# Rotary embedding in quarters, and integer-weight casts on another engine, in a fused attention and FFN kernel

## The reference

```python
qkv = x @ W_qkv                                  # 1024 -> 3 * 1024
bq = bq * dh**-0.5;  bk, bv = look_around(...)   # window before + own window
bq = bq * cos + rotate_half(bq) * sin            # rotary embedding, q and k
bk = bk * cos + rotate_half(bk) * sin
sim = einsum('bhwid,bhwjd->bhwij', bq, bk);  mask;  attn = softmax(sim)
x = layernorm(x + (attn @ bv) @ W_out)
wg, wu, wd = (int32 weights) / 127               # HIDDEN = 3072
x = layernorm(x + (silu(x @ wg.T) * (x @ wu.T)) @ wd.T)
```

## Time and profile before

| | us |
|---|---|
| median of two runs (2235.42 and 2247.68) | 2241.55 |
| the profiled execution | 2229.26 |
| its span on the slowest core (core 1) | 2227.7 |
| spans of the 8 cores | 2201.4 to 2227.7 |
| PE busy in the span | 1789.0 (80%) |
| DVE busy | 630.6 (28%) |
| ACT busy | 528.9 (24%) |
| POOL busy | 345.4 (16%) |

### The profile page before, as it was taken

One profiled execution on the slowest core, in us unless ns is written; L12 is line 12 of the kernel. 1 busy time (PEld: TensorE's weight loads), 2 busy tenths in 40 slices (PEclk: granted clock), 3 DMA queues, 4 the chain that ended last, 5 costly groups with the idle time before them and its releaser, 6 DMA issues.

```text
span 2227.7 us, 27579 instructions; the slowest of 8 cores (2201.4 to 2227.7 us)
## 1 busy us (share of the span) xinstructions
PE 1789.0 (80%) x9568; PEld 789.5 (35%) x9568; DVE 630.6 (28%) x1000; ACT 528.9 (24%) x738; POOL 345.4 (16%) x549
## 2 busy tenths in 40 slices
PE   0075958686877969596599999999999999999992
PEld 0032323233323334243244444434444344444440
DVE  1013232333323232332311333132331423323212
ACT  2134242424233343424110211102111021120200
POOL 0122221313131222221000001020110202002022
PEclk9997989898977889898799999999999999999996
DMA  9874655556554546240424234252342523325251
GB/s 286 256 178 117 181 145 176 156 165 168 149 163 149 170 143 193 77 133 25 156 75 134 66 96 136 90 151 67 105 127 81 156 70 125 105 76 161 71 156 47
DMA packets 156088, 294.21 MB, mean 132 GB/s; under 512 B 22066, under 2 KB 41266, under 8 KB 155954
## 3 DMA queue, kind: packets, MB, share of 16 engines
q1 hardware_dynamic: 91442, 177.06, 27.1%
q10 hardware_dynamic: 46080, 65.03, 9.5%
q0 software_dynamic: 18432, 50.36, 7.5%
HBM read 231.54 MB, written 44.04 MB: 124 GB/s over the span
## 4 chain that ended last, share of the span: by engine, by line
PE 44%; issue 2%; ACT 1%; DVE 1%; DMA 1%; POOL 1%; SPq 0%; DVEq 0%; ACTq 0%; POOLq 0%
PE pg L995 14%; PE pu L1003 14%; PE pd L1044 8%; PE pg L1044 4%; PE pu L1044 4%; DMA wg_sb<-wg_sc 1%; PE pd L884 1%; PE pd L888 1%; DMA wd_buf<-wd_sc 1%; ACT L909 0%; POOL o L956 0%; DVE res L1055 0%; DVE rowsc L904 0%; DVE rows L894 0%; ACT rowsc L909 0%
## 5 line engine op out<-in xcount | busy, mean ns | idle before, releaser
L995 PE MATMUL pg<-y_sb,wg_sb 128*128 128x512 bf16 x1536 | 367.7, 382 | 33.1 <-DVE res L1055 14.9
L1003 PE MATMUL pu<-y_sb,wu_buf 128*128 128x512 bf16 x1536 | 364.5, 380 | 0.1
L1010 ACT ACTIVATE a_sb<-pg,consts 128x512 bf16<-128x512 f32 x192 | 131.2, 687 | 814.9 <-PE pg L995 814.8
L1015 DVE TENSOR_TENSOR h_sb<-a_sb,pu 128x512 bf16<-128x512 bf16 x192 | 131.3, 687 | 516.3 <-PE pu L1003 480.8
L440 PE MATMUL ps_ab<-x,wqk_buf 128*128 128x512 f16 x704 | 170.9, 393 | 126.0 <-ACT x L385 120.7
L995 PEld LDWEIGHTS pg<-y_sb,wg_sb 128*128 128x128 bf16 x1536 | 149.4, 98 | 223.4 <-issue 49.4
L956 POOL TENSOR_TENSOR o<-res,mbc 128x512 f32<-128x512 bf16 x64 | 75.1, 1174 | 933.1 <-ACT mbc L935 917.3
L1003 PEld LDWEIGHTS pu<-y_sb,wu_buf 128*128 128x128 bf16 x1536 | 150.6, 98 | 182.8 <-issue 2.8
L1044 PE MATMUL pd<-h_sb,wd_buf 128*128 128x512 bf16 x768 | 203.1, 387 | 1.9 <-DMA wd_buf<-wd_sc 1.5
L440 PEld LDWEIGHTS ps_ab<-x,wqk_buf 128*128 128x128 f16 x704 | 70.3, 101 | 215.7 <-issue 154.1
L706 PE MATMUL ps_ab<-q_sb,wqk_buf 128*128 128x512 f16 x512 | 128.9, 417 | 13.9 <-DVE q_sb L670 8.4
(11 more groups left out here) (115 smaller groups left out, 1813.8 us busy)
## 6 DMA issues: line engine op xcount, KB each, us to landing
wu_buf<-wu_sc SPq DMA_DIRECT2D x192, 256.0 KB, 2.6
wd_buf<-wd_sc SPq DMA_DIRECT2D x192, 256.0 KB, 3.5
wqk_buf<-wqk_sc SPq DMA_DIRECT2D x128, 256.0 KB, 3.4
x<-x_fm POOLq DMA_DIRECT2D x64, 256.0 KB, 4.8
wqk_buf<-wo_sc SPq DMA_DIRECT2D x64, 256.0 KB, 4.4
out_fm<-o POOLq DMA_DIRECT2D x64, 256.0 KB, 3.9
pin<-wgT ACTq DMA_DIRECT2D x48, 256.0 KB, 4.1
pin<-wu_shuf ACTq DMA_DIRECT2D x48, 256.0 KB, 4.0
```

Of the source, the lines that this page charges most:

```text
L995: g_last = P.op("pe", lambda e, hc=hc, dci=dci, gb=gb, yt=yt: e.matmul(out=pg[gb][:], lhsT=wg_sb[:, dci * HID + hc * 128: dci * HID + (hc ...
L1003: u_last = P.op("pe", lambda e, dci=dci, gb=gb, ub=ub, yt=yt: e.matmul(out=pu[gb][:], lhsT=wu_buf[:, ub * 1024 + dci * 128: ub * 1024 + (d ...
L1010: sl = P.op("act", lambda e, gb=gb: e.activation(out=a_sb[:, gb * 512:(gb + 1) * 512], in_=pg[gb][:], func=AF.Silu, scale=consts[:, 1:2]), ...
L1015: ht = P.op("dve", lambda e, hc=hc, gb=gb: e.tensor_tensor(out=h_sb[:, hc * 512:(hc + 1) * 512], in0=a_sb[:, gb * 512:(gb + 1) * 512], in1 ...
```

## The change

Two things are changed, both in the attention part.

The integer casts of `bg_prep` are no longer shared between DVE and POOL; ACT executes all 144 of them, at the same places of the program.

`rope_pass2` works by quarters: each quarter has its own cosine product, sine product and add, one behind the other, and the cosine product and the four DMAs wait for the eviction of this quarter's second chunk (`qk_ev[9]`, `[11]`, `[13]`, `[15]` for K, `qk_ev[1]`, `[3]`, `[5]`, `[7]` for Q). It still returns one token per half, that of the half's second add, and the operations that use `k_lo` and `q_lo` wait as before. The number of elements and of DMAs stays the same; DVE has 24 rope instructions per tile instead of 16. The changed kernel is two lines shorter, so lines behind the function carry numbers lower by two (L540 becomes L538, L606 becomes L604).

```diff
                 while ip["cv"] < min(prev_ld, prev_st + 4):
                     j = ip["cv"]
-                    eng_c = "dve" if j % 2 == 0 else "pool"
-                    ip["cv_tok"][j] = P.op(eng_c, lambda e, b_=j % 4: e.tensor_copy(
+                    ip["cv_tok"][j] = P.op("act", lambda e, b_=j % 4: e.copy(
                         out=potbf[b_][:], in_=pin32[b_][:]),
                         waits=[ip["ld_tok"][j],
-                               ip["st_tok"][j - 4] if j >= 4 else None], inc=eng_c)
+                               ip["st_tok"][j - 4] if j >= 4 else None], inc="act")
...
-                    for h in range(2):
...
-                        w0 = [ev_half[h]] + w_scr0[h]
-                        tas.append(P.op("dve", lambda e, sl=sl, scl=scl, cos_t=cos_t:
-                                        e.tensor_tensor(out=scl, in0=sl, in1=bc4_(cos_t),
-                                                        op=ALU.mult), waits=w0,
-                                        inc="dve"))
                     for u in range(4):
                         h = u // 2
                         bq = u % 2
                         c0 = u * 1024
-                        rdw = [ev_half[h], st["rot_free"][bq]]
+                        sl = src_sb.ap()[:, c0:c0 + 1024].rearrange(
+                            "p (c n) -> p c n", c=2)
+                        scl = scratch.ap()[:, c0:c0 + 1024].rearrange(
+                            "p (c n) -> p c n", c=2)
+                        wsc = list(w_scr0[0]) if u == 0 else (
+                            list(w_scr0[1]) if u == 2 else [])
+                        ta = P.op("dve", lambda e, sl=sl, scl=scl, cos_t=cos_t:
+                                  e.tensor_tensor(out=scl, in0=sl, in1=bc2(cos_t),
+                                                  op=ALU.mult),
+                                  waits=[ev_q[u]] + wsc, inc="dve")
+                        rdw = [ev_q[u], st["rot_free"][bq]]
                         toks = []
...
-                            waits=[toks[-1], tas[h]], inc="dve")
+                            waits=[toks[-1], ta], inc="dve")
                         st["rot_free"][bq] = tbs[u]
-                    for h in range(2):
...
-                            waits=[tbs[2 * h + 1]] + w_dst, inc="dve"))
+                        tc = P.op("dve", lambda e, sl=sl, scl=scl, u=u,
+                                  dst_qtr=dst_qtr: e.tensor_tensor(
+                            out=dst_qtr[u], in0=scl, in1=sl, op=ALU.add),
+                            waits=[tbs[u]] + (w_dst if u == 0 else []), inc="dve")
+                        tcs[h] = tc
                     return tcs
```

More of the change, by code:

```diff
@@ L531, in build_core_program @@
                 tcs_q = rope_pass2(q_sb, q_hi,
[L532 to L533 removed]
+                                   [x3(q_lo)[:, 0:2, :], x3(q_lo)[:, 2:4, :],
+                                    x3(q_lo)[:, 4:6, :], x3(q_lo)[:, 6:8, :]],
+                                   cos_q, sin_q,
+                                   [qk_ev[1], qk_ev[3], qk_ev[5], qk_ev[7]],
                                    [[tcs_k[0]], [tcs_k[1]]],
```

30 lines of the change are left out of this document (9 added, 21 removed).

## The result

Twelve runs of the changed kernel have a median of 2192.8 us, beside 2241.75 for ten runs of the kernel before. The remaining nine have a median of 2186.05 us, beside 2240.03 for the nine of before, a ratio of 0.976. So the kernel became 2.2 to 2.65% faster: 49 us by the plain medians, 54 by the nine, 59 by the ratio. The interval shows that it is faster, and not that it is so by more than 2%. I had predicted 2154 us, 87.5 us less than before. The direction held.

What follows compares the result with a forecast made beforehand. PE waits at L540 in attention for the late rope chain. Gains of 84.6 us from last V group to first exp and 2.9 at the statistics, 87.5 together, give a median of 2154 us; range 2122 to 2190.

Steps and rivals of the forecast that it cites:

- What bounds the kernel: Attention, L540: PE idles 113.6 us for q_lo because the rope chain is late, behind casts and its own order.
- A: Rival, chance 0.10: ACT shows its new casts at attention's window ends, 34 us back (2188), or 10 us (2164).
- D: Rival, chance 0.04: x loads or DMA congestion hold Q's last quarter; landing 6.6 us loses 34 us (2188).
- B: Rival, chance 0.06: lowered clock spreads, 7.2 us per projection stage; two more 14 us (2168), six 43 us (2197).
- The rope in quarters: Behind the projections only Q's last quarter remains; PE resumes 5.45 us after the last V group, bounds 4.55 and 6.35.
- the landing time: Rope DMAs, fourth issue to sine product: 2.4 us taken, bounds 1.5 and 3.3; 7 us either way on the gain.
- which Q does not feel: POOL's x loads ahead of K's rope stay and hold its start in tile 2 until 378.6, without delaying Q.
- To the first exp: From L540's waiting product to the first exp: 4.2 us with two casts in seven tiles, 3.6 in tile 7.
- One cast leaves the row statistics: DVE's cast ahead of L751 goes, shortening PE's wait there by 0.42 us in seven tiles, 2.9 us.
- Casts on ACT elsewhere: In projections and attention ACT's added casts cost nothing; 10 us if the cover in attention is missing.
- Rival C: Chance 0.03: ACT's casts wait for their loads and hold evictions, exps and PE; 207 us lost, 2361 us.
- ACT idle for pin: Sign that the prediction is wrong: ACT waiting for the integer loads; no size given.

Runs made afterwards that it cites:

- Four buffers: The changed kernel with four rotation buffers instead of two, the two pt_sb tiles added: ratio 0.9568, quickest pair 2124 us on chip B, 2136 on chip A.
- PE and ACT fillers: The kernel before with 40 unread matmuls per tile on PE, ratio 0.9978; separately, with two unread ACT copies per integer cast, ratio 1.01.

## Why the prediction was right, and where it was wrong

**What bounds the kernel: right.** The wait at L540 was the rope chain, held by casts that waited for loads and by the order within the rope. Each half of the change removes its own portion, 43 and 29 us on an undisturbed pair. K's first rotation DMAs now come 13.3 to 13.6 us into the stage on core 5 (13 forecast), and its tiles 1 to 6 follow each other every 108.0 us, where the slowest core before had 118.5 (11 less was forecast); on core 0 it is 116.0.

**That the time lies near the edge of my range is partly luck.** The range was to take in A, D and most of B, each by itself. What came was the larger part of B and a part of D at once, and the two together just fit.

**The rope in quarters, the landing time: mis-sized.** "This time lies between the two states, so I take 2.4 and keep 1.5 and 3.3 as bounds." It was 5.8 and 6.6 us during the projections. For the last quarter alone, 2.9, it was within the bounds. The 3.3 was read in tile 7, which has neither integer loads nor x loads, and I applied it to the seven tiles that have them. The trace of before had a better row, which I did not use: in tile 2 the first four DMAs of K's second pair, issued by 399.54 + 1.96 = 401.50, were used at 407.85, 6.4 us later:

```profile
399.54 3.91 POOL L123 DMA_DIRECT2D rotb<-k_sb  x8 [2.56 <-DVE k_sb L504]
```

```profile
407.85 0.69 DVE L504 TENSOR_TENSOR k_sb<-rotb,sin_k 128x1024 f16<-128x1024 f16 x1 [7.01 <-DMA rotb<-k_sb]
```

The sentence "Only the last quarter of Q remains behind the projections" fell with it: with 6 us of landing and two buffers a pair of quarters takes 9 to 10 us, and the chain was late at V. K was to be done some 10 us before Q's last quarter arrives, about 15 us after POOL can begin; in tile 4 its last add ends 22 us after (564.32 to 586.1) and 5.5 us before (591.5). The late start of K's chain behind the x loads, "which Q does not feel", adds to that in the trace; no run with two buffers took it away. Cost on core 5: 75.5 gained instead of 84.6. Four buffers restore the assumption and the number (79.8 us against 83.9). Rival D named this cause with this landing time, 6.6 us, and put 34 us on it. It cost 9, since the quarter that lands behind V lands in 1.5 to 3.1 us; what the long landings cost is the late issue of that quarter.

**To the first exp: right.** Two casts of 0.62 and 0.61 us stand ahead of the exp. Timeline of ACT, core 5, tile 4:

```profile
604.59 0.62 ACT L338 CAST potbf<-pin 128x512 bf16<-128x512 int32 x1 [0.39 <-ACT q_hi L541]
...
605.12 0.61 ACT L338 CAST potbf<-pin 128x512 bf16<-128x512 int32 x1
605.66 1.11 ACT L604 ACTIVATE pt_sb<-ps_sim,consts 128x1024 f16<-128x1024 f32 x1
```

From the fifth product (601.42) to the exp is 4.24 us; 4.2 was forecast.

**One cast leaves the row statistics: 2.9 us forecast, 0 measured.** PE's wait for this line stayed at 5.4 us on core 5 and is 5.3 on core 0, as on the slowest core before. Timeline of DVE, core 5, before (ahead of tile 4) and after (ahead of tile 3):

```profile
590.96 0.42 DVE L339 CAST potbf<-pin 128x512 bf16<-128x512 int32 x1
591.46 0.74 DVE L751 TENSOR_SCALAR rows<-ps_ab,consts 1x512 bf16<-1x512 f32 x1
```

```profile
442.67 0.74 DVE L749 TENSOR_SCALAR rows<-ps_ab,consts 1x512 bf16<-1x512 f32 x1 [0.41 <-PE ps_ab L737]
```

Where the cast of 0.43 us stood, DVE now idles 0.41 us for PE's last product of the statistics. The cast had been hidden by that wait. I had read who waited for L751 and not what L751 itself waited for.

**Casts on ACT elsewhere: nearly right.** Nothing was forecast, and 10 us at most if the cover was missing. Attention has 1.7 us more on core 5 and some 4 in the mean of the undisturbed cores. The projections have 4.1 more on core 5, but that is only in part ACT: PE waited there once for ACT's eviction of q_sb (1.5 us), and on cores 2, 4 and 6 it waited 3.9 to 5.4 us for weight loads, for which core 5 of before did not wait. Why these loads come later was not tested.

**Rival C, ACT caught by its own loads, came without its price.** ACT did wait for integer loads, 13 times and 40.0 us in all on core 5, up to 4.3 us at once: I had named "ACT idle for pin" as a sign that I was wrong. But all 13 waits lie between the last exp of a tile and the next tile's projections, 4 to 11 us behind that exp. That is where the prediction had said that steps follow each other closely and nothing waits for ACT. The stretch took 1.8 us more than before.

**Rival B, at 0.06, is what happened on the slowest pair.** "7.2 us per projection stage", "the six others 43 us (2197)". Tiles 1 to 6 of core 0 had the lowered clock in their projections, 48.7 to 50.6 us each. Four more such stages than before cost 36.2 us, 9 each, or 8 without the 4 us that core 5 has too, where I had 7.2. Of 88.9 us won behind V the span kept 43.3. My argument against this rival, that the denser second phase runs at the full clock, was sound as an observation and did not exclude it. The step that failed is the clock of the slowest core: the sum left it as it was before, as a term of nothing, and only the rival had a price for it. The Trainium skill (TensorE: Matmul & The Clock Gate, section Seeing it yourself) puts the limit on a whole die, for as long as three of its cores run dense matmuls. Here the level agrees (0.81, and the windows above), and in this profile the extent does not: cores 2 and 3 of the same die were not lowered at the same time, and in the FFN, densest of all, core 0 has 0.98 from 1120 to 2000 us. The three executions of 2374 to 2443 us, in which all four cores of a die were low, may be what the page describes; none of them was profiled, so this stays open.

Whether the change itself makes the stretches more frequent stays open. In the runs of the result its profile has three on one pair and none elsewhere, and its quickest and slowest pairs lay 46 us apart in the median; on chip B it was 32 and 20 us, and the kernel before had 19 there. The ratios are 0.9735, 0.9712 and 0.9686, with intervals that overlap. That the distances on chip A part by where the casts run (23 and 24 us with DVE and POOL, 61 and 63 with ACT) speaks for it; that the change on chip B once lies as low as before, and a kernel with only part of the casts on ACT at 65, speaks for something else beside it. The experiments with PE and ACT fillers name neither as a trigger, and one profile each is little to go by where the same kernel had none on one chip and six on another. No run here controls what sets the stretches off.

So of the 87.5 us forecast: about 9 are missing behind V by the landing time, 2.9 were never there, some 6 are small delays in projections and attention, which leaves 68 to 72 on an undisturbed pair; and on the slowest core more is lost to lowered clocks, 25 us in the profiled execution, and by the ratios of the slowest core (59 us, and 64 and 70 on chip B) 2 to 13 as a rule.

## What to carry to other kernels

- Where each engine executes its list in order, as in this kernel, background work that waits for a load holds everything behind it. Ask of each queue what stands ahead of the operation on the critical chain and what that one waits for; put such work where the next urgent operation comes late. And ask it of the operation whose delay you mean to shorten, too: it may have a second wait just behind the first.
- Take the landing time of a DMA from the traffic that it will run in. A tile without the background loads showed 1.5 to 3.3 us, the busy ones up to 7.6. When a transfer takes longer than the pace at which its sources arrive, the number of buffers sets the time.
- For a kernel on eight cores, read the spans of all cores first. A gain that every core has is seen on the slowest only as far as the clocks allow.

The four-buffer version has the quickest pair of all, 2124 us against 2209 before, and the lowest single time, 2131.88 us; its slowest core was not shown to be faster than that of the change.

## What the runs showed of the hardware that I had not expected

- The lowered clock of TensorE (0.81 granted) came to neighbouring pairs of cores, mostly for about 162 us and beginning 5 to 10 us into a projection stage, and cost some 15 us of span. In the profiles it did not follow the die.
- The landing of four 64 KB copies from SBUF to SBUF, issued by POOL, took 1.5 us when the other traffic was lower (DMA share 0.57; 379.24 + 1.96 to DVE's operation of tile 2 with four buffers at 382.74), 1.5 to 3.3 beside weight loads alone (tile 7), and 2.4 to 7.6 beside weight, integer and x loads.
